# Vision-text layer with soft mixture of experts on one core: paced patches, woven last attention steps, ScalarE's early order, combine with 512 columns

## The reference

```python
h = patchify(x) @ tok_W.T + tok_b                  # 32 x 36 x 256, from 768 pixels a patch
h = concatenate([h, txt], axis=1)                  # 32 x 113 x 256
n = layernorm(h)
q, k, v = rope(n @ Wq.T), rope(n @ Wk.T), n @ Wv.T # 16 heads of 16
h = h + softmax(q @ k.T * 16 ** -0.5) @ v @ Wo.T
n = layernorm(h)                                   # 3616 tokens
logits = n @ phi_w.T + phi_b                       # token x 64 experts x 32 slots
D, C = softmax(logits, over slots), softmax(logits, over experts)
X = tanh(layernorm(clip(D.T @ n)))                 # 64 x 32 x 256, a sum over all tokens
Y = X @ expert_w + expert_b
h = h + C @ Y
```

## Time and profile before

| | |
|---|---|
| median of 3 runs | 988.93 us (988.03 to 990.25) |
| profiled execution, whole | 990.47 us |
| its span, first to last instruction | 988.8 us |
| PE / DVE / ACT / POOL busy | 923.2 / 712.5 / 502.7 / 540.0 us |
| mean granted TensorE clock | 0.965 of full |
| first attention score | 51.48 us |
| last attention score | 308.46 us |
| first DVE work on slot tile 1 / tile 5 | 346.77 / 413.03 us |
| first and last output tile added | 822.34 / 983.50 us |

### The profile page before, as it was taken

One profiled execution on the slowest core, in us unless ns is written; L12 is line 12 of the kernel. 1 busy time (PEld: TensorE's weight loads), 2 busy tenths in 40 slices (PEclk: granted clock), 3 DMA queues, 4 the chain that ended last, 5 costly groups with the idle time before them and its releaser, 6 DMA issues. The chain is left out here.

```text
span 988.8 us, 22780 instructions
## 1 busy us (share of the span) xinstructions
PE 923.2 (93%) x8222; PEld 788.1 (80%) x8222; DVE 712.5 (72%) x1047; ACT 502.7 (51%) x817; POOL 540.0 (55%) x494
## 2 busy tenths in 40 slices
PE   4889999999997858799999999999999989999997
PEld 3778888888885546688888888888888749999997
DVE  1356777777773598899999999999998754454452
ACT  1155555555554244566676667667665253333331
POOL 2265222222221177699999999999998452100100
PEclk9899999999997778899999999999999999999999
DMA  8311111111111042233323322332336995677660
GB/s 315 99 31 43 43 42 42 42 42 42 42 35 39 14 105 55 61 84 97 86 69 87 95 70 73 95 90 63 88 86 239 363 400 202 220 231 240 213 186 17
DMA packets 97907, 110.89 MB, mean 112 GB/s; under 512 B 12180, under 2 KB 89012, under 8 KB 91716
## 3 DMA queue, kind: packets, MB, share of 16 engines
q1 hardware_dynamic: 95908, 105.46, 34.5%
q0 software_dynamic: 1376, 3.70, 1.0%
q10 hardware_dynamic: 576, 1.11, 0.3%
HBM read 72.04 MB, written 38.21 MB: 111 GB/s over the span
## 5 line engine op out<-in xcount | busy, mean ns | idle before, releaser
L1224 PE MATMUL slots_p_sum<-slots_x,slots_disp 128*128 128x256 f32 (+1 forms) x928 | 206.9, 380 | 2.2 <-DVE xacc L933 2.2
L1224 PEld LDWEIGHTS slots_p_sum<-slots_x,slots_disp 128*128 128x128 f32 (+1 forms) x928 | 173.4, 190 | 26.9 <-issue 4.2
L1029 POOL TENSOR_TENSOR slots_comb<-slots_comb,slots_cmax 128x1024 f32<-128x1024 f32 (+1 forms) x58 | 111.7, 1944 | 11.4 <-DVE slots_cmax L908 10.3
L1040 POOL TENSOR_TENSOR slots_comb<-slots_comb,slots_csum 128x2048 f32<-128x2048 f32 (+1 forms) x29 | 104.9, 3619 | 19.1 <-DVE slots_csum L862 19.1
L1251 PE MATMUL slots_logits<-phi_hi,slots_xt_hi 128*128 128x512 f32 (+1 forms) x232 | 84.2, 446 | 19.7 <-DVE slots_xt_lo L888 19.7
L1034 POOL TENSOR_TENSOR slots_disp<-slots_disp,slots_dsum 128x2048 f32<-128x2048 f32 (+1 forms) x28 | 102.1, 3646 | 0.0
L398 POOL TENSOR_TENSOR attend_stack<-attend_rope_a,attend_rope_b 113x128 f32<-113x128 f32 x128 | 54.4, 457 | 80.4 <-DVE attend_rope_b L353 80.4
L1068 POOL DMA_DIRECT2D out<-slots_o x29 | 15.9, 548 | 149.0 <-DVE slots_o L970 149.0
L876 DVE TENSOR_TENSOR slots_disp<-slots_logits,slots_dmax 128x512 f32<-128x512 f32 (+1 forms) x116 | 80.2, 691 | 4.2
L1081 ACT ACTIVATE slots_ct<-slots_p_turn 128x512 f32<-128x512 f32 (+1 forms) x116 | 63.9, 577 | 31.1 <-PE slots_p_turn L1212 31.1
L871 DVE TENSOR_REDUCE slots_dmax<-slots_logits 128x16 f32<-128x512 f32 (+1 forms) x116 | 77.7, 669 | 0.0
(11 more groups left out here) (133 smaller groups left out, 1962.3 us busy)
## 6 DMA issues: line engine op xcount, KB each, us to landing
combine_t<-slots_ct SPq DMA_DIRECT2D x224, 128.0 KB, 2.4
slots_comb<-combine_t SPq DMA_DIRECT2D x14, 1024.0 KB, 5.5
slots_ct<-combine_t SPq DMA_DIRECT2D x14, 1024.0 KB, 6.1
expert_w<-wexp SPq DMA_DIRECT2D x8, 1024.0 KB, 9.9
slots_disp<-wexp SPq DMA_DIRECT2D x8, 1024.0 KB, 14.2
h<-attend_h_out SPq DMA_DIRECT2D x32, 113.0 KB
slots_h_t<-h SPq DMA_DIRECT2D x28, 128.0 KB, 2.3
slots_x<-h SPq DMA_DIRECT2D x28, 128.0 KB, 2.1
```

The source lines that it names most:

```text
L1029: nc.gpsimd.tensor_tensor(m, m, cmax[0:rows, shalf(i)].unsqueeze(2).broadcast_to([rows, SLOTS // 2, EXPERTS]), ALU.subtract).then_inc(csub ...
L1040: nc.gpsimd.tensor_tensor(m, m, csum[0:rows, 1].unsqueeze(2).broadcast_to([rows, SLOTS, EXPERTS]), ALU.mult).then_inc(comb_ok, 1)
L1224: last = nc.tensor.matmul(p_sum[u % 2][:, i, :], disp[d][0:rows].rearrange("p n s -> p (n s)")[:, 128 * e:128 * e + 128], x[d][0:rows], st ...
```

## The change

It has five parts.

1. **Embed.** Tile t's load (t above 2) waits until tile t-2 has landed; the attention weights' loads move from ScalarE's queue into SP's, behind tiles 4, 5 and 6. A zeroed tile is multiplied five times on PE ahead of tile 0. ScalarE now starts, once tile 0's pixels are there, the loads of the identity, the texts of sequences 0 and 1 and the rope tables, then stores tile 0 itself and loads the patches of sequences 0 and 1. The weights' low parts are made by DVE, between the bias additions of tiles 3, 4 and 5, which are all ahead of step -2 now. In DVE's step the embed additions stand behind the norm. The phi weights are loaded by SP ahead of step -1, and their pieces treated in steps 0 to 4; steps 3 and 4 leave the hardware loop.
2. **Last attention steps.** The loads and norms of slot tiles 0 and 1 start behind steps 27 (SP) and 29 to 31 (DVE, GpSimd); tile 0 is turned inside step 31. Steps 32 and 33 are no longer run as such: their parts are called by hand in `rest`, between the four banks of tile 0's logits.
3. **ScalarE in slot steps 1 to 4.** ScalarE does the first copies to `xacc` in DVE's place. Its order becomes: exponentials of `comb`, then the four quarters, then the two copies.
4. **Combine.** `y_hi` and `y_lo` lie side by side, and hi x (y_hi, y_lo) is one product with 512 columns: 15 of them, then 16 lo x y_hi with 256 columns, then the last one. DVE adds the two halves in two instructions.
5. For that, `xacc` and the expert bias lie interleaved block by block, as one tile.

```diff
-    turn = {-4: range(0, 1), -3: range(1, 3), -2: range(3, 5), -1: range(5, 7), 0: range(7, tiles)}
+    turn = {-4: range(0, 1), -3: range(1, 3), -2: range(3, 6), -1: range(6, 8), 0: range(8, tiles)}
...
             for t in range(1, tiles):
+                if t > 2:
+
+                    sp.wait_ge(px_in[t - 2], 16)
                 sp.dma_start(px[:, t], patches[t]).then_inc(px_in[t], 16)
+                if t >= tiles // 2 and t - tiles // 2 < len(loads):
+                    n = t - tiles // 2
+                    sp.dma_start(raw[n][:], loads[n][0]).then_inc(raw_in[n], 16)
+            return
...
+        if b == -4:
+            act.wait_ge(emb_ready, 1)
+            act.dma_start(emb[0:128, :], emb_sb[:, 0]).then_inc(emb_out[0], 16)
...
+        if b == -4:
+
+            pe.wait_ge(warm_ok, 1)
+            for _ in range(5):
+                nc.tensor.matmul(acc[BANKS - 1][:, 0:C], warm[:, 0:128], warm[:], start=True, stop=True)
...
+    def scalar(act, follow, rest):
+        act.wait_ge(begun, 16)
+        act.dma_start(ident[:], identity).then_inc(ident_in, 16)
+        for b in range(2):
+            act.dma_start(h_in[b][PATCHES:T, :], txt[b * WORDS:(b + 1) * WORDS, :]).then_inc(h_ld[b], 16)
+        act.dma_start(cos[:], rope_cos).then_inc(tables_in, 16)
+        act.dma_start(sin[:], rope_sin).then_inc(tables_in, 16)
...
+        def rest(finish, add, low):
+
+
+            low_turned(0, SHORT)
+            dispatch_in(0, 0, SHORT, 0)
+            finish()
+            dispatch_in(0, 0, SHORT, 1)
+            add(BATCH - 2)
+            dispatch_in(0, 0, SHORT, 2)
+            low()
+            dispatch_in(0, 0, SHORT, 3)
+            low_turned(1, 128)
+            add(BATCH - 1)
+            norm(2, 0, 128, 1)
+            combine_max(0, 0, SHORT)
+            norm_end(2, 0, 128)
+            dispatch_sum(0, 0, SHORT)
...
+            if live and filling:
+                for i in range(2):
+                    exp_half(comb[c % 2], shalf, csub_ok, 1, cexp_ok, i)
             if weights:
                 keep_quarter(t - 1, (c + 1) % 2, half(-1), 0)
                 keep_quarter(t - 1, (c + 1) % 2, half(-1), 1)
-                if units:
+                if units and not filling:
                     keep_sum(*units[1])
...
+            if units and filling:
+                for s, u in units:
+                    keep_sum(s, u)
...
+        def rest(turn_values, project_out, turn_back):
+
+
+            multiply_logits(-1, SHORT, [0])
+            turn_values()
+            multiply_logits(-1, SHORT, [1])
+            project_out(BATCH - 2)
+            multiply_logits(-1, SHORT, [2])
+            turn_back()
+            multiply_logits(-1, SHORT, [3])
+            turn_x(0, 0, 128)
+            project_out(BATCH - 1)
+            multiply_logits(0, 128, range(NB))
...
+            for e in range(EB - 1):
+                high_product(e)
+            if static(n) and n == 0:
+                pe.wait_ge(y_hi_ok, EB)
+            for e in range(EB):
+                nc.tensor.matmul(p_o[c % 2][0:rows, 0:C], lo[c % 2][:, e, 0:rows], y_hi[:, e, :], start=False, stop=False)
+            last = high_product(EB - 1)
             last.then_inc(mm_ok, 1)
```

More of the change, by code:

```diff
@@ L144, in tensor @@
             pe.wait_ge(ident_in, 16)
-        if b == -2:
+        if b > -3 and b + 2 < len(loads):
+            pe.wait_ge(lo_done, b + 3)
+        if b == 0:
             pe.wait_ge(lo_done, len(loads))
@@ L237, in wait_for, with steps @@
             eng.wait_ge(which, val(n))
-    def steps(eng, step, enter, follow):
+    def steps(eng, step, enter, follow, last=BATCH + 2):
         def straight(b):
             step(b, lambda n: (b + n) // 2, b % 2, [0 <= b + n < BATCH for n in (3, 2, 1, 0, -1, -2)])
-        for b in range(-3, 3):
+        for b in range(-3, 5):
             if b <= 0:
@@ L249, in steps @@
             straight(b)
-        with eng.Fori(0, (BATCH - 6) // 2) as k:
-            for c in (3, 4):
+        with eng.Fori(0, (BATCH - 8) // 2) as k:
+            for c in (5, 6):
                 step(Count(k, 2, c), lambda n, c=c: Count(k, 1, (c + n) // 2), c % 2, [True] * 6)
-        for b in range(BATCH - 3, BATCH + 2):
+        for b in range(BATCH - 3, last):
             straight(b)
@@ L298, in sync, with vector @@
             follow(sp, b)
-    def vector(dve, follow):
+    def vector(dve, follow, rest):
+        e_vector(dve, -5)
         nc.vector.memset(eps[:], EPS)
@@ L370, in vector @@
         e_vector(dve, -4)
-        steps(dve, step, e_vector, follow)
+        steps(dve, step, lambda dve, b: b == 0 and e_vector(dve, b), follow, BATCH)
+        rest(lambda: finish(BATCH), lambda b: add(b + 2, lambda n: (b + 2 + n) // 2, b % 2, False), lambda: low(BATCH, False))
     def gpsimd(pool, follow):
@@ L471, in scalar, with tensor @@
         e_scalar(act, -4)
-        steps(act, step, e_scalar, follow)
-    def tensor(pe, follow):
+        act.wait_ge(emb_out[0], 16)
+        for b in range(2):
+            act.dma_start(h_in[b][0:PATCHES, :], emb[b * PATCHES:(b + 1) * PATCHES, :]).then_inc(h_ld[b], 16)
+        steps(act, step, e_scalar, follow, BATCH)
+        rest(lambda: keep_values(BATCH), lambda: high(BATCH, False))
+    def tensor(pe, follow, ahead, rest):
         pe.wait_ge(pads_ok, 2)
@@ L520, in step @@
             if finishes:
[L522 to L526 removed]
+                turn_values(b, turns)
             if turns:
@@ L560, in step @@
             if finishes:
-                pe.wait_ge(on_ok, val(b))
-                wait_for(pe, h2_ok, b - 1)
-                pe.wait_ge(v_ok, val(b + 2) if turns else BATCH)
-                for k in range(KC):
-                    last = nc.tensor.transpose(ont_ps[:, k, :], on[:].rearrange("p g j d -> p (g j d)")[:, 128 * k:128 * k + 128],
-                                               ident[0:T, 0:T])
-                last.then_inc(ont_ps_ok, 1)
+                turn_back(b, turns)
+            if isinstance(b, int) and b == BATCH - 1:
+                ahead()
             if normalises:
@@ L585, in tensor @@
         e_tensor(pe, -4)
-        steps(pe, step, e_tensor, follow)
+        steps(pe, step, e_tensor, follow, BATCH)
+        rest(lambda: turn_values(BATCH, False), lambda b: project_out(b + 2), lambda: turn_back(BATCH, False))
     return (sync, vector, gpsimd, scalar, tensor), (phi_lo_ok, PIECES), (qmax_ok, h2_ok, h2_out)
@@ L614, in slots @@
     with ExitStack() as sums:
-        xacc = sums.enter_context(nc.sbuf_tensor("xacc", [128, EB, C], F32))
-        eb = sums.enter_context(nc.sbuf_tensor("expert_bias", [128, EB, C], F32))
-    y_hi, y_lo = [sb(f"y_{part}", [128, EB, C], F32R) for part in ("hi", "lo")]
+        sums_bias = sums.enter_context(nc.sbuf_tensor("sums_bias", [128, EB, 2, C], F32))
+    xacc, eb = sums_bias[:, :, 0], sums_bias[:, :, 1]
+    y_parts = sb("y_parts", [128, EB, 2, C], F32R)
+    y_hi, y_lo = y_parts[:, :, 0], y_parts[:, :, 1]
     behind = [sb(f"disp{i}", [128, EXPERTS, SLOTS]) for i in range(TG + 1, RING)]
```

320 lines of the change are left out of this document (189 added, 131 removed).

## The result

The changed kernel takes 961.12 us (median of 4 executions, 957.64 to 961.52), the kernel before 989.33 beside it (988.03 to 990.25): a ratio of 0.9704, 95% interval 0.969 to 0.9718. A second session gave 958.84 (5 executions, 956.16 to 963.31), ratio 0.9685 (0.966 to 0.9709). The nine executions together have a median of 960.85. The forecast was 961.6. Its total is right. Of its terms the start is far off, the border and the combine are too small, and the errors cancelled: that the total came within 1 us is luck.

A forecast was written before the change was run, and what follows sets the result against it. No engine bounds the whole span; PE and GpSimd bound the slots' loop, PE the combine. Start 11.0, border 8.7, slot steps 6.5, loop -1.3 and combine 2.4 sum to 27.3 us gained: 961.6 us median, range 954 to 970.5.

The forecast's parts named there:

- I take 2.2 us: Start: tile 0's store, issue to its loads' issue, would take 2.2 us (bounds 1.7 and 6.2) instead of 6.17.
- I take 2.8: Start: the first sequences' loads would take 2.8 us from their issue (bounds 1.7 and 3.6) instead of 3.6.
- I take the clock as staying up: Start: with PE idle only 2 or 3 us, tiles 3 and 4 would run at full clock, gaining 2.5 us.
- GpSimd's 3.1 us: Start: DVE's 4.03 us wait for the deviation would lose 3.1 us once GpSimd no longer splits weights.
- the start keeps its wait: Rival: store and loads stay 6.2 and 3.6 us, PE loses its clock; start gains 1.7, total 971; chance 0.10.
- The load's 4.0 us: Border: issuing slot tile 0's load three steps earlier would let DVE's last attention maximum start 4.0 us sooner.
- the clock stays up at the border: Rival: full clock through step 31 at the border brings 4.6 us more, total 957; chance 0.10.
- lost into the loop: Step 5: PE's turn of the next tile waits for a later third-quarter eviction; 1.3 us lost (bounds 0 and 2).
- half clock takes the gain: Rival, slot steps 1 to 4: ScalarE or half clock leaves a gain of 1 instead of 6.5, total 967; chance 0.12.
- the wide product, 233.8 ns: Combine: one 512-column product at 233.8 ns replaces two at 120.0, each pair 6.2 ns cheaper, 2.9 us in all.
- The split of weights on ScalarE: Start: splitting attention weights before the first eviction costs nothing behind PE's tiles 3 to 5; without that cover, 2 us.
- the rival "slower": Loop: GpSimd's `xacc` additions in two runs take longer; 0.57 us more each loses the whole gain; chance 0.04.

The follow-up runs named there:

- the run with the copy on the chip: Changed kernel, but sequence 0's rows of tile 0 copied on the chip by VectorE, sequence 1's by one transfer from the chip's own buffer: 956.27 us.
- the faster kernel: Changed kernel with first two sequences' rows kept on chip, ScalarE splitting only q/k weights before the first eviction, q/k weights requested behind tile 2's pixels: 952.43 us.

## Why the prediction was right in sum, and where it was wrong

**Start: wrong, 3.95 us for 11.0, outside its own bounds.** By the prediction's own test (a first score above 44 us would be wrong) this step failed: 47.53. The working failed at "I take 2.2 us" for the store and "I take 2.8" for the loads. The 2.2 leaned on the median of the earlier trace rows, and eight of its nine stores were issued long after tile 0's, from 21.18 us on. The text named the right suspects, pixels and weights in flight, and then took the separate queue and the pacing as a cure. Two tiles and a weight matrix in flight are enough for 5.62 and 4.21 us. The run with the other loads held back shows it from the other side: 2.11 and 2.38, 0.1 and 0.4 below the forecast's values, and a first maximum at 42.07, 10.5 us ahead of the 52.61 of the kernel before.

The second failed step is "I take the clock as staying up". PE idled 7.62 us instead of "2 or 3" and fell to half clock (0.50 at 24 to 28 us), so tiles 3 to 5 took 10.59 us instead of 7.95. A shorter idle time would not have saved all of it: in the run with the loads held back PE idled 2.28 us, and they took 9.63. What held: GpSimd's 3.1 us (the wait of 4.03 became 1.06, 3.0 less), which is all that PE's first turn gained (26.33 to 23.39), and tile 0's time, with a term of 0.1 rather than 0.5 in this profile. Nearest was the rival "the start keeps its wait" (1.7 us gained there, at a chance of 0.10, by which the whole would have been 971).

What the prediction had no term for: this start has two forms some 4 us apart. Where tile 0's matmuls reach the full rate early, the addition comes 1 us sooner, and the store then takes 2.93 to 3.89 us in the five early profiles, against 5.03 to 5.62 in the three late ones. The forecast's "if the clock is up by 8 it ends 0.5 early, if it comes up as late as before, it ends 1.5 late" described the spread of the addition and let it end there.

**Border: direction and mechanism right, 13.1 for 8.7, near the upper bound.** The load's 4.0 us are borne out (a wait of 3.50 where the load was made late again). The mis-sized terms are the two behind it. From the last score to VectorE's first bank the prediction had 322.3 - 308.46 = 13.8 us, and it took 315.59 - 303.97 = 11.6; for the list from there to tile 1's first bank it had 15.8, and it took 13.6. The prediction took the clock as low until the third bank; the windows give 0.95 at 300 to 310 us, 0.71 at 310 to 320 and 1.00 behind that, and PE's score itself ran at full rate (1.06 us instead of 1.88). By the runs, 3.3 us go with the load's wait and lay behind it, the weave brings 2.6 to 3.5, and some 3.3 are left, for which the old order of banks and last products is the likely cause. The size, 4.4 us more, is that of the rival "the clock stays up at the border" (chance 0.10, 4.6 us more), but only half of its mechanism came: the clock stayed up through the score and fell to 0.50 at 310 to 315 us. Why VectorE's list was 2.2 us shorter has no run of its own.

**Slot steps 1 to 4: right, 8.1 for 6.5, and 1.7 lost into the loop for 1.3.** Net 6.35 for 5.2, within the bounds; undoing it cost 6.9. The mechanism is the forecast one: the cycles took 14.1, 14.1, 15.0 and 15.0 us for 14.4, 14.4, 15.3 and 15.3, and VectorE's wait for `xt_hi` in the last two was 0.67 for 0.9. The rival that half clock takes the gain did not come, though a stretch of half clock on step 5 costs 2.3 to 2.6 us in some executions.

**Combine: direction right, size half.** 5.21 in 27 tiles less 0.29, 4.9 for 2.4; the upper bound was set at the value itself and was broken. The mis-sized term is the wide product, 233.8 ns from the earlier trace rows. Those rows are the logits, whose products follow each other more slowly. The combine's own rate is 228.7, so a pair saves 2 x 120.0 - 228.7 = 11.3 ns instead of 6.2. The Trainium skill (TensorE: Matmul & The Clock Gate, "Wait — 56ns, not 53.3ns?") has about 2.5 ns for the fixed cost of the matmul that goes; the runs with narrow products show some 11 to 12 for a pair, and the measurement decides. They don't show that all of it is a cost of the matmul, since a weight load goes with it. The second addition cost 0.4 us at the end (5.71 us from the last tile's first addition to the end, instead of 5.30), as forecast.

**Steps costed at nothing.** The phi loads and pieces and the unrolled steps cost nothing: first to last score took 256.44 for 256.98. The split of weights on ScalarE cost nothing in this kernel either. The loop step is the same (tile turns 14.45 us apart), and GpSimd's additions to `xacc` are not slower, so the rival "slower" did not come. In the run with the copy on the chip, where the sequence arrives in time, the split does bind: the eviction waited 6.7 us for it, and PE 3.18 behind tiles 3 to 5. Its cover, PE's tiles 3 to 5, was right only as long as the start was late.

**The sum.** Against the forecast: -7.1 at the start, +0.5 in the loop of attention, +4.4 at the border, +1.2 in slot steps 1 to 5, +2.5 in the combine, +0.2 between; together +1.7 in the spans. The range held because the terms erred to both sides, as it assumed, but that they left only 1.7 us in the sum is luck; the start alone at 4 with the rest as forecast would have been 968.7.

## What to carry to other kernels

Price a small transfer on the critical path by what flies beside it at that time, not by its median elsewhere: here 2.1 us became 5.6 although it had another issuing queue, and holding the large loads back (7 us) or keeping the data on the chip (8.4 us with the two moves behind it) helped. A wait that leaves PE idle can have a second price, the half clock of the work behind it; at the border what came behind was as large as the wait (3.3 beside 3.5). Take the rate of an instruction from a stretch where it runs in long rows without a gap, and give its bound room on both sides.

## What the runs showed of the hardware that was not expected

- The issue of one small load (the sine table) held ScalarE for 2.25 us with paced loads, 5.19 in the faster kernel and 7.37 without pacing. What stands behind a transfer's issue on a computing engine waits too.
- Equal kernels differ by up to 7 us (956.16 to 963.31) with places that can be named: 4 us at the start, with 6 or 10 of tile 0's matmul records between 6 and 8 us, and 2.3 to 2.6 in slot step 5 by a stretch of half clock.
- Behind 7.62 us without PE work at the start the clock stood at 0.50 (24 to 28 us, first profile), and behind only 2.28 us it fell too (0.73 at 20 to 24 us, loads held back). With no such stretch tiles 3 to 5 took 7.95 us, 2.6 less than in the first profile.
- A wide fp32r product costs 228.7 ns in the combine, and 233.8 for each of the logits' eight, with the same columns and the same full clock. Why the logits are slower is open.
